# Seven edge passes of a graph network: tiles grouped by four in seven of eight steps, single in the eighth

## The reference

```python
# CompGCN, twice
comp = x[src] * rel_emb[l][ridx]
agg_f = jax.ops.segment_sum(comp * norm * fmask, dst, num_segments=N_NODES)
agg_b = jax.ops.segment_sum(comp * norm * bmask, dst, num_segments=N_NODES)
# GAT, three times, 8 heads
logits = jax.nn.leaky_relu(al_s[src] + al_d[dst], LRELU_SLOPE)
m = jax.ops.segment_max(logits, dst, num_segments=n_nodes)
e = jnp.exp(logits - m[dst])
denom = jax.ops.segment_sum(e, dst, num_segments=n_nodes)
out = jax.ops.segment_sum(e / denom[dst] * xw[src], dst, num_segments=n_nodes)
```

## Time and profile before

| | |
|---|---|
| median of 3 runs | 11693.11 us (11682.03 to 11700.05) |
| the profiled execution | 11695.19 us, its span 11693.4 us |
| mean granted TensorE clock | 0.622 of full speed |
| busy | PE 6135.8 us (52%), PEld 4863.7, DVE 4364.6 (37%), ACT 1969.3 (17%), POOL 6088.9 (52%) |
| instructions of PE, DVE, ACT, POOL | 40035, 13034, 5277, 6396 |
| DMA | 1092.81 MB in 774630 packets, mean 93 GB/s |

### The profile page before, as it was taken

The page is one execution under the profiler, slowest core; times in us unless marked ns, Lnnn a source line. Parts: engine busy times, 40 slices in busy tenths (PEclk is TensorE's granted clock), DMA queues, the critical chain, the costliest instruction groups (busy, mean ns, idle before and its releaser), DMA issues. The chain is left out here.

```text
span 11693.4 us, 143529 instructions
## 1 busy us (share of the span) xinstructions
PE 6135.8 (52%) x40035; PEld 4863.7 (42%) x40036; DVE 4364.6 (37%) x13034; ACT 1969.3 (17%) x5277; POOL 6088.9 (52%) x6396
## 2 busy tenths in 40 slices
PE   3545455555544345565556556655555555555454
PEld 3444444555322223343434344444344444444444
DVE  4333322222211113555555455554444444433233
ACT  1222210100211112111112111111211111111111
POOL 4666656666466663444443444444355555355554
PEclk6565655555676766666667566666655555556666
DMA  4444422222222232333332333333223333233333
GB/s 124 141 141 139 138 69 78 79 77 70 68 73 74 73 75 77 107 106 107 107 106 80 111 107 106 105 106 107 63 79 80 79 79 79 63 97 96 94 97 83
DMA packets 774630, 1092.81 MB, mean 93 GB/s; under 512 B 389184, under 2 KB 429440, under 8 KB 774160
## 3 DMA queue, kind: packets, MB, share of 16 engines
q0 software_dynamic: 233760, 503.07, 17.2%
q1 hardware_dynamic: 540784, 588.70, 17.0%
HBM read 1016.16 MB, written 75.04 MB: 93 GB/s over the span
## 5 line engine op out<-in xcount | busy, mean ns | idle before, releaser
L681 POOL DMA_INDIRECT gat_rows<-xw_table,gat_index x2736 | 2593.8, 948 | 2958.4 <-DVE gat_msg_s L1763 1822.8
L1850 PE MATMUL bank<-gat_msg_s,gat_hot 128*128 128x264 f32 (+1 forms) x5472 | 2077.5, 542 | 680.9 <-DVE gat_msg_s L1763 438.8
L1850 PEld LDWEIGHTS bank<-gat_msg_s,gat_hot 128*128 128x128 f32 x5472 | 1443.5, 301 | 1138.9 <-issue 905.6
L681 POOL DMA_INDIRECT att_rows<-pre_table,att_index x912 | 862.6, 946 | 814.0 <-ACT att_index L671 518.2
L681 POOL DMA_INDIRECT msg_rows<-pre_table,msg_index x912 | 865.1, 949 | 639.3 <-ACT msg_index L671 371.2
L681 POOL DMA_INDIRECT gcn_rows<-in_x,gcn_index x912 | 878.0, 963 | 564.1 <-ACT gcn_index L671 284.0
L893 PE MATMUL bank<-gcn_rel,gcn_rhot 100*128 100x64 f32 x3648 | 701.6, 344 | 890.0 <-issue 698.0
L681 POOL DMA_INDIRECT gcn_rows<-x_table,gcn_index x912 | 885.8, 971 | 542.3 <-issue 278.6
L893 PEld LDWEIGHTS bank<-gcn_rel,gcn_rhot 100*128 100x128 f32 x3648 | 678.9, 269 | 928.5 <-issue 862.7
L730 PE MATMUL bank<-gcn_msg_s,gcn_hot 128*128 128x128 f32 x3648 | 814.6, 374 | 448.8 <-issue 441.8
L730 PEld LDWEIGHTS bank<-gcn_msg_s,gcn_hot 128*128 128x128 f32 x3648 | 707.1, 277 | 512.5 <-issue 512.0
(11 more groups left out here) (285 smaller groups left out, 10049.3 us busy)
## 6 DMA issues: line engine op xcount, KB each, us to landing
gcn_ids<-rel_rows SPq DMA_DIRECT2D x228, 400.0 KB
gat_hot_half<-edge_hots SPq DMA_DIRECT2D x342, 256.0 KB
gat_dhot<-dst_hots SPq DMA_DIRECT2D x342, 256.0 KB
gcn_dst<-dst_rows SPq DMA_DIRECT2D x114, 512.0 KB
gat_rows<-xw_table,gat_index POOLq DMA_INDIRECT x2736
edge_hots<-gcn_hot_half SPq DMA_DIRECT2D x114, 256.0 KB
dst_hots<-gcn_dhot SPq DMA_DIRECT2D x114, 256.0 KB
gcn_hot_half<-edge_hots SPq DMA_DIRECT2D x114, 256.0 KB
```

The source lines that it names most:

```text
L681: pool.indirect_dma_start(self.rows[n.q][:, j, :], None, self.table, bass.IndirectOffsetOnAxis(ap=self.index[n.q][:, j:j + 1], axis=0))\
L1850: ins = pe.matmul(sum_ps[g][:, 0:wide], hot[n.q][:, g * GROUP + j, :], msg[q][:, g * GROUP + j, :], start=j == 0, stop=j == GROUP - 1)
```

## The change

Tiles of 128, not groups of 512, become the unit of the layout. Each pass is cut into turns of 8 steps; in seven of them a step is 2 groups of 4 tiles as before, and the fourth (`MIXED = 3`) holds 8 single tiles, each with a block of its own. A block's whole groups of 4 fill the former, 182 groups in all (`PURE`); what is left of each block goes tile by tile into the latter. The tiles come to 832, in 104 steps (13 turns), where 228 groups were 912 tiles in 114 steps. The number of gathers, products and messages of a step stays as it was; a mixed step has 8 sums, 8 additions onto `acc`, 8 updates of the maxima and 8 block numbers in place of 2.

```diff
 PAIR = 2
 BATCH = PAIR * GROUP
-NG = -(-((E + NB * (GE - 1)) // GE) // (2 * PAIR)) * 2 * PAIR
-STEPS = NG // PAIR
-KG = -(-NG // P)
-NGP = KG * P
-NIP = NGP * GROUP
+TURN_STEPS, MIXED = 8, 3
+TURNS = -(-((E + NB * (P - 1)) // P) // (TURN_STEPS * BATCH))
+STEPS = TURNS * TURN_STEPS
+TILES = STEPS * BATCH
+KT = -(-TILES // P)
+NTP = KT * P
+PURE = TURNS * (TURN_STEPS - 1) * PAIR
+assert PURE <= -((NB * (GROUP - 1) * P - E) // GE)
+BLOCKS_OF = [BATCH if r == MIXED else PAIR for r in range(TURN_STEPS)]
+TURN_BLOCKS = sum(BLOCKS_OF)
+ONCE = [1] * TURN_STEPS
...
-
-    def count(self, per, plus):
+    def __init__(self, turn, step):
+        self.turn, self.ahead, self.r = turn, step // TURN_STEPS, step % TURN_STEPS
+        self.q = self.r % RING
+        self.mixed = self.r == MIXED
+        self.blocks = BLOCKS_OF[self.r]
...
-def sum_groups(pe, hot, msg, banks, width, summed):
-
-    for g in range(PAIR):
-        for j in range(GROUP):
-            ins = pe.matmul(place(banks, g, width), hot[:, g * GROUP + j, :], msg[:, g * GROUP + j, 0:width],
-                            start=j == 0, stop=j == GROUP - 1)
+def sum_groups(pe, n, hot, msg, banks, width, summed):
+
+    for g in range(n.blocks):
+        tiles = [g] if n.mixed else range(g * GROUP, (g + 1) * GROUP)
+        for j in tiles:
+            ins = pe.matmul(place(banks, g, width), hot[:, j, :], msg[:, j, 0:width], start=j == tiles[0], stop=j == tiles[-1])
...
                     for g, b in enumerate(ids):
                         top = m.top[:, ds(b, 1), :]
                         own = slice(g, g + 1)
-                        dve.wait_ge(topped, n.total(PAIR, g + 1))
+                        dve.wait_ge(topped, n.before(BLOCKS_OF, g + 1))
                         dve.tensor_tensor(new[q][:, own, :], top, near[q][:, own, :], ALU.max).then_inc(raised, 1)
-                        dve.wait_ge(raised, n.total(PAIR, g + 1))
+                        dve.wait_ge(raised, n.before(BLOCKS_OF, g + 1))
                         dve.tensor_tensor(fall[q][:, own, :], top, new[q][:, own, :], ALU.subtract).then_inc(fallen, 1)
-                        dve.wait_ge(fallen, n.total(PAIR, g + 1))
+                        dve.wait_ge(fallen, n.before(BLOCKS_OF, g + 1))
...
-                def add(g):
+                    dve.tensor_copy(kept[q][:, 0:n.blocks, :], fade[q][:, 0:n.blocks, :]).then_inc(fade_kept, 1)
+
+                def add(half):
                     def part(n):
                         q = n.of(TWO)
-                        b = (earlier or blocks_of(nc, dve, m, n))[g]
-                        if g == PAIR - 1:
+                        ids = earlier or blocks_of(nc, dve, m, n)
+                        dve.wait_ge(fade_kept, n.total(1, TWO + 1))
+                        for g in halves(n)[half]:
+                            dst_acc = m.acc[:, ds(ids[g], 1), 0:wide]
+                            by_head = dst_acc.rearrange("p o (h e) -> p (o h) e", h=HEADS)
+                            wait_past(dve, added, n.before(BLOCKS_OF, g))
+                            dve.tensor_tensor(by_head, by_head, kept[q][:, g, :].unsqueeze(2).to_broadcast([P, HEADS, c + 1]), ALU.mult)\
+                                .then_inc(scaled, 1)
+                            dve.wait_ge(summed, n.before(BLOCKS_OF, g + 1))
+                            dve.wait_ge(scaled, n.before(BLOCKS_OF, g + 1))
+                            dve.tensor_tensor(dst_acc, dst_acc, sum_ps[g % TWO][:, 0:wide].unsqueeze(1), ALU.add).then_inc(added, 1)
...
-                def sums(g):
+                def sums(half):
                     def part(n):
                         q = n.of(TWO)
                         pe.wait_ge(msg_made, n.total(1, RING + 1))
-                        pe.wait_ge(added, n.total(PAIR, g + 1))
-                        for j in range(GROUP):
-                            ins = pe.matmul(sum_ps[g][:, 0:wide], hot[n.q][:, g * GROUP + j, :], msg[q][:, g * GROUP + j, :],
-                                            start=j == 0, stop=j == GROUP - 1)
-                        ins.then_inc(summed, 1)
+                        for g in halves(n)[half]:
+                            wait_past(pe, added, n.before(BLOCKS_OF, g + 1 - TWO))
+                            tiles = [g] if n.mixed else range(g * GROUP, (g + 1) * GROUP)
+                            for j in tiles:
+                                ins = pe.matmul(sum_ps[g % TWO][:, 0:wide], hot[n.q][:, j, :], msg[q][:, j, :],
+                                                start=j == tiles[0], stop=j == tiles[-1])
+                            ins.then_inc(summed, 1)
...
+        halves = lambda n: (range(PAIR), range(PAIR, BATCH)) if n.mixed else (range(1), range(1, PAIR))
```

The message pass is changed as well: the 8 sums of a mixed step come in three shares (3, 3, 2) that take turns in two banks, and its additions stand ahead of the preactivations in DVE's order:

```diff
+                    ids = blocks_of(nc, dve, m, n)
+                    for k, groups in enumerate(shares(n)):
+                        dve.wait_ge(summed, n.before(SUMS, k + 1))
+                        for g in groups:
+                            dve.wait_ge(added, n.before(BLOCKS_OF, g + 1))
+                            dst = m.acc[:, ds(ids[g], 1), 0:HID + 1]
+                            dve.tensor_tensor(dst, dst, place([bank_of(n, k)], g - groups[0], HID + 1).unsqueeze(1), ALU.add)\
+                                .then_inc(added, 1)
...
-                pipeline(dve, (0, angles, TIMES), (1, preactivations), (3, adds))
+                pipeline(dve, (0, angles, TIMES), (3, adds), (1, preactivations))
...
+                    for k, groups in enumerate(shares(n)):
+                        s = sum(SUMS[:n.r]) + k - TWO
+                        wait_past(pe, added, n.at(TURN_BLOCKS, upto[s] + 1 - (TURN_BLOCKS if s < 0 else 0)))
+                        for g in groups:
+                            tiles = [g] if n.mixed else range(g * GROUP, (g + 1) * GROUP)
+                            for j in tiles:
+                                ins = pe.matmul(place([bank_of(n, k)], g - groups[0], HID + 1), hot.full[q][:, j, :],
+                                                msg[q][:, j, 0:HID + 1], start=j == tiles[0], stop=j == tiles[-1])
+                        ins.then_inc(summed, 1)
```

More of the change, by code:

```diff
@@ L283, in _ @@
                 dve.wait_ge(turned, 1)
[L284 to L285 removed]
+                for there, here in tables():
+                    dve.tensor_copy(there, here)
             @block.tensor
@@ L604, in at @@
                 if 0 <= t - lag < (count[0] if count else STEPS):
-                    part(Step(None, (t - lag) // per_turn, (t - lag) % per_turn, per_turn))
+                    part(Step(None, t - lag))
     at(range(head))
-    with eng.Fori(head // per_turn, whole // per_turn) as turn:
-        for r in range(per_turn):
+    with eng.Fori(head // TURN_STEPS, TURNS) as turn:
+        for r in range(TURN_STEPS):
             for lag, part, *count in parts:
                 if not count:
-                    part(Step(turn, (r - lag) // per_turn, (r - lag) % per_turn, per_turn))
-    at(range(whole, STEPS + last))
+                    part(Step(turn, r - lag))
+    at(range(STEPS, STEPS + last))
 def in_turn(first, second):
@@ L711, in load, with widen @@
         return part
-    def widen(self, act, summed, per):
+    def widen(self, act, summed, sums):
         def part(n):
@@ L744, in wait_added @@
 def wait_added(eng, n, added):
-    eng.wait_ge(added, n.total(PAIR, PAIR))
+    wait_past(eng, added, n.before(BLOCKS_OF, 1, 1))
 def place(banks, g, width):
-    if not isinstance(banks, list):
-        return banks[:, g * width:(g + 1) * width]
-    return banks[g][:, 0:width]
+    each = CHUNK // width
+    return banks[g // each][:, g % each * width:(g % each + 1) * width]
 def compgcn_pass(nc, m, a, layer, table):
@@ L1711, in maxima @@
                     first = n.turn is None and n.total(1, 0) == 0
-                    ids = blocks_of(nc, dve, m, n, 0 if first else PAIR)
-                    earlier[:], ids = ids[:-PAIR], ids[-PAIR:]
+                    ids = blocks_of(nc, dve, m, n, not first)
+                    earlier[:], ids = ids[:-n.blocks], ids[-n.blocks:]
+                    all = slice(0, n.blocks)
                     dve.wait_ge(picked, n.total(1, RING + 1))
@@ L2190 @@
     arrays["dst_runs"] = np.concatenate([dst[0:P * DC].reshape(P, DC), dst[DC::DC].reshape(P, 1)], axis=1)
+    slot = np.arange(NTP).reshape(KT, P).T
+    turn, step, tile = slot // (TURN_STEPS * BATCH), slot // BATCH % TURN_STEPS, slot % BATCH
+    mixed, later = step == MIXED, (step > MIXED) * BATCH
+    order = np.where(mixed, PURE * GROUP + turn * BATCH + tile, slot - turn * BATCH - later)
+    order = np.where(slot < TILES, order, 4 * TILES)
+    offset = np.where(mixed, 0, tile % GROUP * P)
+    limit = np.where(mixed, E - P, E - GE + offset)
+    arrays["slots"] = np.ascontiguousarray(np.stack([order, limit, offset], axis=1).astype(np.float32))
     half = P // 2
```

308 lines of the change are left out of this document (161 added, 147 removed).

## The result

The new kernel takes 10,892.15 us, median of 4 runs (10,883.47 to 10,906.57), where the old one takes 11,696.58 (4 runs): a ratio of 0.9315, 95% interval 0.9303 to 0.9326, 804 us less. The forecast was 11,264 us with a range from 10,950; the direction was right, the size was not.

A forecast was written before the change was run, and what follows sets the result against it. The prediction took a closed DVE-PE circle to bound GAT steps, and POOL's gather floor plus PE stalls the others. 11,695.2 - 960 + 421 + 105 + 5 = 11,266, less 2.1, about 11,264 us; range 10,950 to 11,570.

The forecast's parts named there:

- Ten steps less: All seven passes: ten steps of each removed at that pass's mean step time, 960 us less.
- What a mixed step adds in the GAT: Three GAT passes, 13 mixed steps each: more maxima, additions and wider small operations on DVE, paid in full, 421 us more.
- Outside the GAT: CompGCN, message and attention passes, 13 mixed steps each: PE's sums wait for additions, 105 us more, bounds 0 and 250.
- Once: Outside the steps: more table columns, seven edge-field gathers instead of two, less wide operations; 5 us more, bounds 0 and 20.
- Rival A: GAT: PE's pace ends the logits wait, which absorbs up to 5.0 us; elsewhere POOL's floor hides all; 10,990 us, chance 0.22.
- Rival B: Longer loop fetched anew, each jump back stalling an engine, 2.85 us per wait; 11,375 to 11,486 us, chance 0.13.
- C: Mixed GAT steps: each DVE-PE bank hand-over costs 2 to 4 us, 24 us more per step; 11,779 us, chance 0.10.
- D: No gain: PE's stalls go by time, removed steps save only 707 us, costs at upper bounds; 11,813 us, chance 0.05.
- One reading of the earlier trace: First two GAT passes: PE's and DVE's busy times were read as a little above POOL's.

The follow-up runs named there:

- group 4: Slower chip, dst_gather held for POOL's issued gathers: old kernel 11,913.9 us; new 11,065.9; new without six maxima updates and addition pairs 11,015.1; new with four added DVE operations 11,117.0.
- pure8: New kernel's code with only whole groups, 120 steps a pass, turns of 8 steps, result differs; 9,181.5 us on a faster chip.
- pure4: New kernel's code with only whole groups, 120 steps a pass, turns of 4 steps, result differs; 9,175.8 us on a faster chip.
- before_held: Old kernel, PE's dst_gather in the GAT passes waiting for a small POOL write behind the step's gathers; 11,913.9 us, ratio 1.0074, on a slower chip.
- before_again: The old kernel unchanged, run once more on a faster chip for its trace; 8,734.7 us.
- before_tied: Old kernel, PE's dst_gather in the GAT passes waiting for a semaphore POOL's queue raises behind the gathers; 8,737.4 us on a faster chip.

## Why the prediction was wrong

- *Ten steps less, 960 us:* right on the chip of the forecast (961). On the faster kind they are worth 705, since a step is at POOL's floor there.
- *What a mixed step adds in the GAT, 421 us:* the step that failed. It measured 105. The sizes of its parts held (0.71 us for a block's maxima, 1.10 for an addition), but the sentence "what DVE gets more in this circle is paid in full" was false: the circle that sets the step goes through POOL's gathers, and the maxima and six of eight additions lie beside it. The sentence's own proviso, that something else than the start that DVE gave might end the wait ahead of the logits, came true. A row that pointed to it was in hand: POOL waits for the messages, so a burst begins right behind them, and 0.8 + 9.7 + 1.7 + 1.6 + 2.35 is a step of 16.1 us (14.7 where the 1.7 is 0.2; the mean is 15.6). I took these waits for a consequence of DVE's circle, and never laid the burst's end beside the logits' start. That the circle goes through the gathers on the slower kind is shown by the traces and by group 4's differences; on the faster kind the sentence was nearer the truth, since work behind the messages was paid at 505 us for 560.
- *Outside the GAT, 105 us:* 20, nearly all in the message pass (27). There PE's sums wait for additions as forecast (L1327, 270 us of idle time; in the old kernel none is put down to additions), and the pass pays 2.1 us a turn, not 4; in CompGCN and attention the additions are hidden.
- *Once, 5 us:* 33. The time from the last gather of a GAT pass to its last addition grew from 39 to 47 us in the first pass on the first chip, and from 25 to 42 on the faster kind; what the rest is was not tried.
- *Rival A* (absorbed, 10,990 us, a chance of 0.22) was the right one in that the wait swallowed the work, and still 98 us too high, as it let 5.8 us of each mixed step stand where 2.7 did. Its cause, PE's own pace, is only half of it: the wait ends at a fixed distance from POOL's last gather.
- *Rival B:* the new loop is indeed fetched at each turn. The Trainium skill's rule ("Runtime: NRT & Kernel Launch", section "Instruction fetch mechanics"), that a taken branch out of the resident pages stalls for a fetch, agrees with the 2.81 us at a turn's begin. The size of the stall was right (2.85 us); what it costs depends on its place: nothing that can be seen in the GAT passes of the first chip, 6 us in pure8 over pure4, and by the estimate above up to 100 us in the new kernel on the faster kind.
- *Rivals C and D* didn't occur: additions follow each other every 1.10 us, and on the first chip the four rounds of a turn that are farthest from the mixed step average 15.7, 15.6 and 14.5 us in the three GAT passes, where the old kernel's steps average 15.6, 15.6 and 14.3.
- One reading of the earlier trace rows was off without entering the sum: in the first two GAT passes PE's busy time stands 143 and 173 us above POOL's, which isn't a little.

What isn't settled: why on the slower kind of chip the semaphore that the logits wait for comes so late, and PE's small products behind it one at a time, while POOL gathers. Where dst_gather is held until the gathers are issued (before_held), the semaphore comes 0.65 us after the last product's modelled end and the late singles are gone from the GAT, so it is tied to the gathers' time; the cause stays open. The lower granted clock (0.62 against 0.68) is no full account of it: PE's busy time in the old kernel differs by 447 us between the two kinds, the span by 2,972. The version with late gathers, which would have tried it, ran only on the faster kind.

## What to carry to other kernels

A wait between two engines that is much longer than the work between them belongs to a third: look for what ends at a fixed distance ahead of the waiting instruction in many steps, and take the circle from there before pricing added work. Work is priced by its place in that circle: 1.8 us a step cost 505 us in one setting and 51 in the other. And the same change was worth 6.9% on one kind of chip and 3.7% on the other, so a gain that comes from filling a wait should be measured where the wait is short as well. The same holds for a price: a pair that shows a cost of nothing shows it for its own bottleneck only.

## What the runs showed of the hardware that was not expected

- The old kernel took 8,736 to 8,743 us on four chips, and 11,693 and 11,831 us in two other comparisons, with the same instruction counts; the granted TensorE clock was 0.68 of full speed in the former and 0.61 to 0.62 in the latter. In the old kernel's slower trace single PE products follow each other 0.7 to 2.5 us apart; in the faster one's GAT step that was looked at (3900 to 3912 us of before_again) none do.
- In the old kernel's first GAT pass the logits, which wait for the semaphore behind dst_gather's last product, start 5.5 us (median) after that product's modelled end on the slower chip, and 0.04 us after it on the faster one.
- A semaphore that POOL's queue raises behind gathers is raised before they are issued (12.2 us before the last one starts, in before_tied); one raised by a small write on the engine behind them is raised after the last one (in one step of before_held at 4753.98 us, where the last gather starts at 4752.91).
- A loop of 4 steps drew no instruction packets in the steady stretch; one of 8 steps drew 74 on q14 in the first GAT pass, with 2.8 us without work on DVE at a turn's begin. It cost 6 us in 9,176 where POOL set the pace, and, estimated from the trace, up to 100 us in 8,417 where DVE did.
